# Second attention: the small extra matmuls of an item issued between its scores and its maxima

## What is computed

```python
Q = (hs @ q_w + q_b).reshape(B, S, H, HD).transpose(0, 2, 1, 3)
K = (hs @ k_w + k_b).reshape(B, S, H, KPH).transpose(0, 2, 1, 3)
V = (hs @ v_w + v_b).reshape(B, S, H, KPH).transpose(0, 2, 1, 3)
scores = jnp.einsum('bhsk,bhtk->bhst', Q[..., :KPH], K) / math.sqrt(KPH)
attn = jax.nn.softmax(scores, axis=-1)
ao = jnp.einsum('bhst,bhtv->bhsv', attn, V)
ao = ao.transpose(0, 2, 1, 3).reshape(B, S, H * KPH)
mla_out = jnp.concatenate([ao, zeros], axis=-1) @ o_w + o_b
```

## Time and profile before

| | before |
|---|---|
| median of 3 runs | 1699.26 us (1698.1 to 1699.73) |
| profiled execution | 1698.94 us, of which its span is 1697.1 us |
| TensorE matmul (PE) busy | 1612.6 us, 95% |
| VectorE (DVE) busy | 1432.8 us, 84% |
| ScalarE (ACT) busy | 1211.1 us, 71% |
| GpSimd (POOL) busy | 453.1 us, 27% |
| first and last exponential of the second attention | 797.7 and 1466.1 us |
| first and last maxima read in its loop (L1726) | 797.6 and 1441.8 us |

### The profile page before, as it was taken

How to read it: one execution, slowest core, us unless ns; L and a number is a source line. 1 busy time by engine, 2 the same in 40 slices (tenths; PEclk the granted TensorE clock), 3 DMA queues, 4 the chain that set the end, 5 groups by cost and what they waited for, 6 DMA issues and landing times. The chain is left out here.

```text
span 1697.1 us, 37918 instructions
## 1 busy us (share of the span) xinstructions
PE 1612.6 (95%) x14716; PEld 702.4 (41%) x14716; DVE 1432.8 (84%) x2059; ACT 1211.1 (71%) x1210; POOL 453.1 (27%) x562
## 2 busy tenths in 40 slices
PE   4999999999999999987999999999999999889995
PEld 2444444444444444442233333333332332556774
DVE  6777778888888888997999999999999999177888
ACT  3776666666667666654887888788878888756776
POOL 2311112333232333341333322322232333220004
PEclk9999999999999999995999999999999999989998
DMA  6311110111101110011012000200020010000001
GB/s 152 70 37 38 37 37 21 37 37 37 37 36 37 37 37 25 17 32 32 15 38 51 14 14 14 51 14 14 14 51 14 14 38 2 15 8 8 13 12 50
DMA packets 46737, 53.38 MB, mean 31 GB/s; under 512 B 9293, under 2 KB 33565, under 8 KB 46622
## 3 DMA queue, kind: packets, MB, share of 16 engines
q1 hardware_dynamic: 45572, 50.06, 10.2%
q10 hardware_dynamic: 1050, 1.73, 0.4%
HBM read 15.59 MB, written 10.49 MB: 15 GB/s over the span
## 5 line engine op out<-in xcount | busy, mean ns | idle before, releaser
L1726 DVE TENSOR_REDUCE arena<-psum 128x2 f32<-128x1024 f32 x490 | 585.6, 1220 | 38.0 <-PE psum L1337 31.9
L1509 ACT ACTIVATE arena<-psum 128x1024 f32<-128x1024 f32 x512 | 523.1, 1025 | 122.0 <-PE psum L1311 108.1
L713 ACT ACTIVATE arena<-psum 128x2048 f32<-128x2048 f32 (+1 forms) x160 | 274.0, 1712 | 231.2 <-PE psum L548 231.0
L1326 PE MATMUL psum<-arena 128*32 128x256 f32 x4096 | 327.8, 392 | 1.4 <-ACT arena L1523 0.7
L805 POOL TENSOR_SCALAR_AFFINE_SELECT arena<-arena 128x512 f32<-128x512 f32 (+1 forms) x160 | 151.7, 965 | 520.5 <-ACT arena L713 520.5
L567 PE MATMUL psum<-arena,hs 128*64 128x512 f32 (+3 forms) x1536 | 283.0, 496 | 0.1
L548 PE MATMUL psum<-arena 64*128 64x512 f16 (+3 forms) x2304 | 216.1, 325 | 3.4 <-DVE arena L851 3.4
L1311 PE MATMUL psum<-arena 32*128 32x512 bf16 x1024 | 199.5, 387 | 4.2 <-DVE arena L1726 3.0
L1337 PE MATMUL psum<-arena 32*128 32x512 bf16 x980 | 189.7, 384 | 5.6 <-ACT arena L1509 1.9
L851 DVE TENSOR_TENSOR arena<-arena 128x1024 f16<-128x1024 f32 x64 | 80.3, 1255 | 99.7 <-ACT arena L692 99.7
L567 PEld LDWEIGHTS psum<-arena,hs 128*64 128x64 f32 x1536 | 96.0, 136 | 141.3 <-issue 125.2
(11 more groups left out here) (213 smaller groups left out, 2085.6 us busy)
## 6 DMA issues: line engine op xcount, KB each, us to landing
arena<-arena SPq DMA_DIRECT2D x30, 512.0 KB, 2.9
arena<-arena SPq DMA_DIRECT2D x46, 128.0 KB, 2.2
arena<-latent_q SPq DMA_DIRECT2D x64, 64.0 KB, 2.0
arena<-latent_k SPq DMA_DIRECT2D x64, 64.0 KB, 2.1
arena<-arena SPq DMA_DIRECT2D x60, 64.0 KB, 2.4
X<-in_L_attn_states SPq DMA_DIRECT2D x4, 512.0 KB, 6.1
out_x<-X SPq DMA_DIRECT2D x4, 512.0 KB, 3.3
latent_q<-arena SPq DMA_DIRECT2D x16, 96.0 KB, 2.2
```

What stands on the lines that cost most here:

```text
L713: nc.scalar.activation(probs[g], SC[:, :, 0:WIDTH[g]], ACT.Exp, scale=DH ** -0.5).then_inc(exp_done, 1)
L1326: last = nc.tensor.matmul(OT[ROWS * c:ROWS * (c + 1), h * HALF // 2:(h + 1) * HALF // 2], v_cols[par][:, kt, 2 * pr + i, :], e_probs[u % 4 ...
L1509: nc.scalar.activation(e_probs[u % 4], src, ACT.Exp, scale=KD ** -0.5).then_inc(e_done, 1)
L1726: nc.vector.tensor_reduce(half_tops[:, kh, qt, 2 * pr:2 * pr + 2], src.rearrange("p (i c) -> p i c", i=2), AX.X, ALU.max).then_inc(top_don ...
```

## The change

In `group` of the second attention's TensorE program the call of `spare` moves from behind `maxima` to ahead of it, right behind `scores`. The wait for `e_done` moves behind `spare` with `maxima`, and the waits inside `spare` now stand ahead of `maxima`. No instruction is added or taken away; the other four engines' orders are the same.

```diff
                     scores(par, u, slot(n, u, 0))
+                    spare(b, gi, u, last)
                     g, m = divmod(LEAD + u, ITEMS)
                     if not (last and g):
                         if m == 0:
                             pe.wait_ge(qk_in[1 - par], 16 * 2 * GH * (GROUPS // 2 * b + (gi + 1) // 2 + 1))
                         upto(pe, e_done, ITEMS * n + u)
                         maxima(n + g, (par + g) % 2, m, slot(n, u, 1))
-                    spare(b, gi, u, last)
                     if u >= 2:
                         values(n, par, u - 2)
                     elif at_least(n, 1):
                         values(n - 1, 1 - par, ITEMS + u - 2)
```

## The result

| | before | changed |
|---|---|---|
| median of 7 runs | 1699.37 us (1698.10 to 1699.92) | 1733.85 us (1723.80 to 1765.99) |
| ratio | | 1.0187 (95% interval 1.0173 to 1.0201) |
| profiled execution | 1698.94 us | 1765.99 us |

The change made the kernel slower, as forecast, but by twice the forecast 16.6 us, and outside its range. It also made the time uncertain: seven runs of before lie within 2 us, seven of the changed kernel within 42. The ratio leaves out the two longest runs; the median of the other five is 1731.33 us. One of the two, 1765.99 us, is the profiled one. The others left no trace, only a mean granted clock: 0.968 to 0.975 in those five against 0.945 in the profiled one and 0.978 before. So the trace shows more of the loss than a usual run has.

The account below looks back on a forecast made before the run. The prediction took the chain scores, exponential, maxima, values, scores, mostly TensorE, to set the pace. Its terms 2.6 + 2.6 + 3.8 + 6.4 + 1.2 = 16.6 us gave 1715.9 us, range 1706 to 1726 us.

Parts of the forecast that it names:

- the gap: Step g from scores to maxima before the change; moving a piece that waits for nothing costs 0.32 - g per item.
- s = 0.32, and d' = d: After the move, scores to piece (s) takes 0.32 us, piece to maxima (d') as long as piece to values before (d).
- The first rival: Cheaper hand-overs let pieces fill the wait for the exponential; 0.10 less at each gives 1683.5 us; chance 0.03.
- Runs at 6 and 22: Runs of four pieces from these items: six of `queries_keys` lose 2.6 us, nine of single transposes 2.6 us.
- Runs at 14: Twelve runs: the first piece waits for L1735, +0.32 each, 3.8 us; the three other items lose 6.4 us together.
- Sixty single pieces: Pieces at items 4, 12, 20 and 28, mean gap taken as 0.30, cost 60 x 0.02 = 1.2 us.
- I expect the granted clock to stay at 1.00.: TensorE's clock stays at the 2.4 GHz level despite its longest new pause, in item 14, twice the 0.36 of before.
- VectorE as the one that sets the pace: Rival: scores wait for VectorE's reductions, so TensorE's losses vanish in that wait; no change, 1699.3 us; chance 0.05.
- does not catch up: Rival: item 14's reduction starts 1.15 us later and VectorE passes that on, sum 26.6, 1725.9 us; chance 0.08.

Follow-up runs that it names:

- all_but_14: The changed order, but the piece of item 14 stays behind the maxima; median 1716.14 us, ratio 1.0131.
- only_14: The kernel before, with only the piece of item 14 moved ahead of the maxima; median 1704.69 us, ratio 1.0042.
- runs_15_17: The kernel before, with the pieces of items 15 to 17 moved ahead of the maxima; median 1704.57 us, ratio 1.0041.
- moved_l1735_early: The changed kernel, with VectorE's L1735 one place earlier, behind the reduction of item 12; median 1708.43 us, ratio 1.0056.
- pieces_14_17: The kernel before, with the pieces of items 14 to 17 moved ahead of the maxima; median 1723.99 us, ratio 1.0163.
- pieces_12_14: The kernel before, with the pieces of items 12 and 14 moved ahead of the maxima; median 1707.77 us, ratio 1.0072.
- first_of_runs: The kernel before, with L1735 one place earlier and only the pieces of items 6, 14 and 22 ahead of the maxima; median 1690.95 us, ratio 0.9960.
- before_l1735_late: The kernel before, with VectorE's L1735 one reduction later, behind that of item 14; median 1750.96 us, ratio 1.0319.
- before_l1735_early: The kernel before, with VectorE's L1735 one place earlier, behind the reduction of item 12; median 1693.70 us, ratio 0.9978.

## Why the prediction was wrong, and where it was right

The direction was right, and so was the reason given for it: between scores and maxima there is mostly no hole to fill, and a piece put there costs 0.32 less the gap.

- **s = 0.32, and d' = d.** Right. In the changed kernel scores to piece is 0.32 wherever nothing is waited for, and piece to maxima is what piece to values was: 0.42 for L1294. The first rival, cheaper hand-overs, was wrong: in item 6 of group 2 the piece's weight load starts at 890.87, only 0.01 us ahead of its matmul, and the step from scores is 0.32 all the same.
- **Runs at 6 and 22: 5.2 us.** Measured 5.3 in all_but_14 (items 6 to 9: 3.1, items 22 to 25: 2.2).
- **Runs at 14: 3.8 + 6.4 us.** Measured 3.8 for the first item (only_14) and 6.6 for the others (runs_15_17).
- **Sixty single pieces: 1.2 us.** Mis-sized. In moved_l1735_early, where all are moved and no clock falls, they cost 3.9 us (items 12: 1.8, items 20: 0.7, items 28: 1.8, items 4: -0.4), of which the items between them give 0.7 back. The gaps alone, 0.32 - g summed over the trace of before, come to 1.3 us, as forecast. The sum supposed that they wait for nothing; `turn_tops` waits for L1610, whose wait had been hidden by the gap and the maxima. This is most of the difference between 16.6 and 18.9 us.
- **"I expect the granted clock to stay at 1.00."** This is the step that failed. It was worth 14 to 16 us in the median and 47 in the profiled execution. The pause in item 14 was forecast at the right place and length (0.76 us, twice the 0.36 of before; measured 0.79), but its effect on the clock was put at nothing, without a reason. The rows showed the stage at one density of work only, and nothing in them said how far it was from a fall. Without this step the forecast would have been near: 16.6 us against the 18.9 that the move costs at full clock, which would be 1718 us and inside the range.
- **VectorE as the one that sets the pace, or does not catch up.** Both wrong. VectorE stood idle 105.9 us ahead of L1726 (38.0 before), nearly all of it for the maxima, so TensorE was the slower one. That the reduction of item 14 starts a microsecond late had no further cost in only_14, whose stage is longer by 12 x 0.32 and nothing else.

**What brings the clock down.** The runs show that it is not one place. The one kernel with all pieces moved and no wait in item 14 (moved_l1735_early) had no fall, and neither had only_14, with a wait of 0.77 us and the rest as before. Such a wait is enough in some of the groups when item 12 is changed too, in every run when items 15 to 17 are (at least, no run of pieces_14_17 is under 1719 us, where full clock would give 1708), more still when all are, and in nine of twelve groups when it lasts 1.65 us with nothing moved. So a longer pause does it alone, and a shorter one does it together with the changed items beside it. What in these items counts is argued and not shown. They keep scores and maxima from running side by side, which is also what costs the time at full clock; then both losses would have one cause, and the pause would decide where the second strikes. That no fall came in only_14 (first set of runs) and some did in pieces_12_14 (second set) could also come from the chips; within the second set alone, first_of_runs had no fall and pieces_12_14, pieces_14_17 and before_l1735_late had them.

The Trainium skill ("TensorE: Matmul & The Clock Gate", A second HAM failure mode: psum-queue depth-cycling) tells of a kernel in which frequent short idle times between groups of matmuls made the clock swing between its levels. The runs agree in part: pauses of 0.79 us went with five falls in the changed kernel, and pauses of 0.77 us with none in only_14. The prediction did not weigh this.

Open: why a fall comes in one group and not in the next with the same pieces, and how long it lasts (3 to 38 us here, and other groups in other runs). The runs do not settle it.

## What to carry to other kernels

Putting work "into the wait" of an in-order engine pays only in the instances where the wait exists: read the gap of every kind of instance, not of the typical one, since neighbours that use different rows of the array may run side by side and a piece between them undoes that. Before an instruction with a wait is moved ahead of ready work, ask what covered the wait; moving the producer (L1735, one place earlier on VectorE) was worth more than any order of the waiting side. And on TensorE new idle time can have a second price: here a sum made at full clock missed about half of the median's loss. Where a change adds to a pause or thins the work around it, look at the granted clock by stretches and at the spread of the runs, not only at the sum.

## What the runs showed of the hardware that I had not expected

- TensorE's granted clock fell to 1.2 GHz in a stage in which TensorE was busy 97% of the time, behind pauses of 0.79 us in the changed kernel and 0.76 us in pieces_14_17; behind the pauses of 0.77 us in only_14 it did not. Each fall cost 0.37 to 0.40 us per us that it lasted, for an item then takes longer by more than half (group 8: 58.5 us instead of 44.1), and one lasted 38 us although TensorE did not pause in it.
- Pauses of TensorE behind VectorE or GpSimd, on the other hand, cost about their length and no more where no fall followed: 12 x 0.32 us in only_14 for pauses that were 0.41 us longer; 12 x 0.43 us gained in before_l1735_early, where pauses of 0.36 us went away.
